# Both softmax types in 64-row tiles of TensorE, in a differential-attention block with routed experts

## Chip, cores, metric

One Trainium2 chip, one core of it. The metric is the device time of one launch in microseconds (us), median of three runs. Five engines work side by side: TensorE (PE; its weight loads are listed as PEld), VectorE (DVE), ScalarE (ACT), GpSimd (POOL) and SyncE (SP), whose queue starts most transfers (SPq). All times below are us of the profiled execution's own clock unless marked otherwise.

## The reference, cut to what matters

```python
x = X                                             # 32 batches x 256 rows x 128
h = layernorm(x) * (1 + ca) + sa                  # modulation per batch
Q, K, V = h @ W_q.T, h @ W_k.T, h @ W_v.T         # 16 heads, each 2*8 wide
A1 = Q[..., :8] @ K[..., :8].T / sqrt(8)          # the two softmax types
A2 = Q[..., 8:] @ K[..., 8:].T / sqrt(8)          # both with a causal mask
attn = softmax(A1) - lam * softmax(A2)
O = attn @ V
O = O / rms(O) * rms_scale * 0.2
x = x + ga * (concat(O) @ W_o.T)
h = layernorm(x) * (1 + cb) + sb
x = x + gb * top2_of_8_experts(h)                 # silu(h Wg) * (h Wu), then Wd
```

## The kernel before

The program has three stages: setup, attention over 32 batches, then the experts over 136 tiles of 128 routed rows. Attention is written as a software pipeline by hand. In iteration i every engine runs 16 head steps s = 0 to 15 and works at the same time on several batches: row maxima of batch i+1 (`b1`), exponentials and products with the values of batch i (`b2`), and earlier and later stages (projection of `bA` = i+2, outputs of `bC` = i-1, output projection of `bW` = i-2, routing of `bR` = i-3). What stands in a step is written out in the code of each engine; each engine executes strictly in that order, and semaphores (`wait(engine, event, batch, count)`) tie the engines together.

**Units.** The scores of a batch are computed in 24 units of one PSUM bank (128 x 512 fp32), numbered n = 0 to 23. An even step has one unit, an odd step two. They are computed twice. First for the row maxima: PE writes `p_max` (two banks), DVE takes the maxima (L1166, L1169), and the causal mask is added by one more matmul with the identity (L786, L795). Then, an iteration later, for the exponentials: PE writes `p_exp` (three banks), with minus the maximum as further rows of the product, ACT takes the exponential into `probs` (L988), POOL clears what the mask forbids (L1402). A query or key of 8 numbers is split into bf16 parts laid out as 6 slots, 48 rows. The queries of both types stand below each other (96 rows in `qt`), and `kt` has the keys of each type with zeros in the other type's rows. So one matmul works on 96 or 100 rows of which half are zeros.

**Values and outputs.** `outputs` (L835) multiplies a head pair g (0 to 7) of `probs` with `v` in four 32-column tiles of PE; pair g is visited at step 2g+3, the last one in step 1 of the next iteration. ACT copies each two pairs from `p_out` to `ot` (L978, `copy_outputs`, in steps 6, 10, 14 and 2), and PE turns them (L845, `outputs_to_rows`, in steps 11 and 14 for heads 0 to 7 and in steps 4 and 5 of the next iteration for heads 8 to 15).

**The path of the maxima.** For unit 0 of the next iteration SP does one after the other: wait for `l_ready` (POOL's L1408, `low_part`, step 6), nine stores of the parts (L707, L711), wait until they are saved, seven loads of queries and keys (L734, L740, `load_unit`), the store of the turned maxima (L747), wait until it is saved, and the load of them into `qt` (L750). PE's first exponential unit (L812) waits for that load, `nm_loaded`.

**Setup.** POOL fills `v` and zeroes `kt` (L1393); DVE waits for all 20 constant loads, two of them rows of ones for `kt` (L680).

## Time and profile before

| | us |
|---|---|
| three runs | 1588.79, 1586.29, 1580.92 |
| median | 1586.29 |
| the profiled execution: its time / its span | 1589.78 / 1588.0 |
| setup and filling of the pipeline, to about | 170 |
| steady attention iterations, about | 170 to 1030 |
| the rest of attention, tables, experts, final sum | 1030 to 1588 |

The page gives each engine's busy share over the whole span: PE 86%, weight loads 67%, DVE 74%, ACT 56%, POOL 55%. In the steady stretch the shares are higher and close to each other. A busy engine in such a pipeline may still be one that is waited for, and a short wait may be the one that sets the period, so the rows further down are read iteration by iteration. A line number with a matmul stands for a group; "96*128" are the rows and columns of the weights, "96x256" the streamed operand.

### The profile page before, as it was taken

The numbers are of one execution on the slowest core, as the hardware profiler recorded it, in microseconds if no ns is written. First come the engines' busy times: TensorE is split into PE (matmuls) and PEld (weight loads), VectorE is DVE, ScalarE is ACT, GpSimd is POOL, SyncE is SP. The second block draws the span as 40 slices with busy tenths as digits, with TensorE's granted clock in tenths as the row PEclk, the third lists the DMA queues.
The fourth block names the chain that finished last, engine by engine and source line by source line (L and its number), as shares of the span: only waits on it lengthen the run. The fifth ranks groups of instructions, "written<-read, shape, count | busy, mean of one in ns | idle before, by whom it ended". The sixth has DMA issues, their size and how long they took to land. (4 is left out here: it accounts for less than half of the span.)

```text
span 1588.0 us, 42685 instructions
## 1 busy us (share of the span) xinstructions
PE 1366.6 (86%) x13344; PEld 1063.3 (67%) x13345; DVE 1180.9 (74%) x3082; ACT 885.0 (56%) x1918; POOL 868.0 (55%) x1279
## 2 busy tenths in 40 slices
PE   1499999999999999999999999962599999999950
PEld 1266777767777776777777676641588888888850
DVE  4567888888888888788888887866666666666647
ACT  1166777777777777777777777652133333333310
POOL 2045577677767767676776776663233333333334
PEclk9999999999999999999999999985799999999985
DMA  6433443444344354444434533300211111111139
GB/s 213 123 100 83 129 118 94 118 118 114 103 126 121 92 133 110 103 110 118 122 88 120 128 98 90 87 24 14 59 48 43 46 43 42 46 43 45 42 94 295
DMA packets 176591, 152.61 MB, mean 96 GB/s; under 512 B 21491, under 2 KB 159097, under 8 KB 176036
## 3 DMA queue, kind: packets, MB, share of 16 engines
q1 hardware_dynamic: 159096, 123.07, 30.1%
q0 software_dynamic: 8448, 16.93, 3.3%
q10 hardware_dynamic: 8880, 10.49, 1.9%
q8 instruction: 92, 1.51, 0.4%
q14 instruction: 75, 0.61, 0.1%
HBM read 89.37 MB, written 61.55 MB: 95 GB/s over the span
## 5 line engine op out<-in xcount | busy, mean ns | idle before, releaser
L988 ACT ACTIVATE probs<-p_exp 128x512 f32<-128x512 f32 x768 | 446.5, 603 | 183.6 <-PE p_exp L812 164.3
L1402 POOL TENSOR_SCALAR_AFFINE_SELECT probs<-probs 128x256 f32<-128x256 f32 (+1 forms) x768 | 365.4, 485 | 286.4 <-ACT probs L988 278.3
L1166 DVE TENSOR_REDUCE mx<-p_max 128x2 f32<-128x512 f32 x512 | 351.4, 687 | 169.9 <-PE p_max L786 168.9
L647 POOL DMA_INDIRECT pair_out<-on,v x136 | 133.6, 982 | 284.7 <-ACT on L557 279.3
L784 PE MATMUL p_max<-kt,qt 96*128 96x256 bf16 x1024 | 198.6, 275 | 40.5 <-DMA kt<-k_parts 19.7
L835 PE MATMUL p_out<-probs,v 128*32 128x256 f32 (+1 forms) x4096 | 221.0, 333 | 14.0 <-POOL probs L1402 7.5
L812 PE MATMUL p_exp<-qt,kt 100*128 100x256 bf16 x1024 | 196.7, 273 | 16.8 <-DMA qt<-max_parts 14.0
L621 DVE TENSOR_TENSOR ot<-ot,p_max 128x512 f32<-128x512 f32 x136 | 93.5, 688 | 125.8 <-PE p_max L508 106.5
L1169 DVE TENSOR_REDUCE mx<-p_max 128x4 f32<-128x512 f32 x256 | 173.2, 676 | 2.1 <-PE p_max L795 2.0
L835 PEld LDWEIGHTS p_out<-probs,v 128*32 128x32 f32 x4096 | 112.4, 109 | 85.4 <-POOL probs L1402 24.4
L1449 POOL DMA_INDIRECT rows_sorted<-h,idx x128 | 137.4, 1074 | 50.7 <-ACT probs L988 28.6
L557 ACT ACTIVATE on<-p_exp,v 128x128 f32<-128x128 f32 x136 | 50.3, 370 | 195.7 <-PE p_exp L539 195.7
L539 PE MATMUL p_exp<-wd,rest 128*128 x1088 | 143.9, 275 | 0.9 <-ACT on L557 0.9
L784 PEld LDWEIGHTS p_max<-kt,qt 96*128 96x128 bf16 x1024 | 89.3, 100 | 81.5 <-DVE mx L1166 25.6
L786 PE MATMUL p_max<-mask,idb 128*128 128x256 bf16 x512 | 141.1, 276 | 0.0
L551 ACT ACTIVATE ot<-p_exp 128x512 f32<-128x512 f32 x136 | 81.6, 600 | 95.3 <-PE p_exp L508 95.3
L539 PEld LDWEIGHTS p_exp<-wd,rest 128*128 128x128 f32 x1088 | 132.2, 192 | 1.3 <-issue 1.3
L812 PEld LDWEIGHTS p_exp<-qt,kt 100*128 100x128 bf16 x1024 | 98.6, 99 | 36.7 <-DMA qt<-max_parts 18.9
L978 ACT ACTIVATE ot<-p_out,out_scale 128x256 f32<-128x256 f32 x256 | 107.1, 475 | 0.0
L792 PE MATMUL p_max<-kt,qt 96*128 96x128 bf16 x1024 | 101.5, 222 | 4.4 <-DVE mx L1166 2.0
L1408 POOL TENSOR_TENSOR part_l<-rest,part_m 128x512 bf16<-128x512 f32 x64 | 74.2, 1160 | 51.5 <-ACT part_m L1004 51.5
L818 PEld LDWEIGHTS p_exp<-qt,kt 100*128 100x128 bf16 x1024 | 79.8, 98 | 30.8 <-issue 1.1
(169 smaller groups left out, 2757.9 us busy)
## 6 DMA issues: line engine op xcount, KB each, us to landing
qt<-q_parts SPq DMA_DIRECT2D x64, 384.0 KB
q_parts<-part_h SPq DMA_DIRECT2D x96, 128.0 KB, 2.0
kt<-k_parts SPq DMA_DIRECT2D x128, 96.0 KB
v<-rows_sorted SPq DMA_DIRECT2D x136, 65.0 KB, 1.8
q_parts<-part_m SPq DMA_DIRECT2D x64, 128.0 KB, 2.0
kt<-k_parts SPq DMA_DIRECT2D x128, 64.0 KB
qt<-pair_out SPq DMA_DIRECT2D x32, 256.0 KB, 5.4
mods<-mod_rows SPq DMA_DIRECT2D x32, 192.0 KB
```

What stands on the lines that cost most here:

```text
L539: m = nc.tensor.matmul(p_down, hid_t[:, jd.c % 2, f * P:(f + 1) * P], wd[:, bass.ds(w0 + f * P, P)], start=(f == 0), stop=(f == FCH - 1))
L647: nc.gpsimd.indirect_dma_start(pair_out, bass.IndirectOffsetOnAxis(rows_in[:, j.slot, DIM:DIM + 1].bitcast(U32), 0), rows_out[:, j.slot, : ...
L784: nc.tensor.matmul(p_max[:, bank, t * SEQ:(t + 1) * SEQ], qt[0:QK_ROWS, slot, h8, P:SEQ], kt[0:QK_ROWS, slot, t, h8, :], start=(t == 0), s ...
L786: m = nc.tensor.matmul(p_max[:, bank, :].rearrange("p (t k) -> p t k", t=2)[:, :, P:SEQ], idb[:], mask4[:, 0:2, :], start=False, stop=True)
L812: m = nc.tensor.matmul(p_exp[:, bank, t * SEQ:(t + 1) * SEQ], kt[0:ALL_ROWS, slot, t, h8, 0:P], qt[0:ALL_ROWS, slot, h8, :], start=True, s ...
L835: m = nc.tensor.matmul(p_out[32 * j:32 * j + 32, g % 2, SEQ - n:SEQ], v[:, b.par, tile, 2 * g + j // 2, :], src, start=(tile == 0), stop=( ...
L978: m = nc.scalar.activation(ot[:, q // 2, 2 * (q % 2) + k, :], p_out[:, k, :], ACT.Copy, scale=out_scale[:, g:g + 1])
L988: nc.scalar.activation(probs[:, g % 2, k, :], p_exp[:, k, :], ACT.Exp, scale=SCALE).then_inc(exp_done.sem, 1)
L1166: m = V.reduce_max(mx[:, w, 1, :, h8:h8 + 1].rearrange("p t o -> p (t o)"), p_max[:, bank, :].rearrange("p (t k) -> p t k", t=2), AX.X, ne ...
L1169: m = V.reduce_max(mx[:, w, 0, :, h8 - 1:h8 + 1], p_max[:, bank, :].rearrange("p (t h k) -> p t h k", t=2, h=2), AX.X, negate=True)
L1402: G.affine_select(out=blocks, in_=blocks, compare_op=ALU.is_ge, fill=zero, base=0, pattern=[[0, 2 if k < 2 else 4], [1, P]], channel_multi ...
L1449: G.indirect_dma_start(rows_sorted, bass.IndirectOffsetOnAxis(idx[:, bR.par, k:k + 1].bitcast(U32), 0), h2[:, bR.par, k // NT, k % NT, :], ...
```

## The change

1. **Layout.** Each softmax type gets its own 64 rows of `qt` and `kt` (`LANE = 64`): 48 rows of parts, 2 `EDGES` rows, 2 rows of minus the maximum. `kt` has no second copy per type and no zeros any more. The edge rows add -1e30 in the one 64 x 64 block of each diagonal 128 x 128 block that lies wholly above the diagonal.
2. **Units.** A unit now holds one type: two heads of it (k = n % 6 below 4), or four heads' second-row blocks (k = 4, 5). The mask is two matmuls of 64 rows with triangular 64 x 64 blocks. `scores` interleaves, instruction by instruction, the maximum unit of one type (in one 64-row tile of PE) with the exponential unit of the other type (in the other tile).
3. **Values.** `probs` holds four heads (`quad`) per buffer; pair g is visited at step 2g+5, so pairs 6 and 7 are visited in steps 1 and 3 of the next iteration.
4. **Copies.** `copy_outputs` moves from steps 6, 10, 14, 2 to steps 8, 12, 0, 4, and the first `outputs_to_rows` from step 11 to step 12. The one in step 4 stays.
5. **Transfers.** `load_unit` issues eight loads instead of seven (two of queries, 48 rows each), `move_max` two stores (32 rows of 256 B) and two loads instead of one of each.
6. **Setup.** The zeroing of `kt` goes; the ones are no longer among the constants DVE waits for (18 instead of 20). Ten loads of ones and edge rows come in their place, eight of them behind a wait for POOL; PE waits for all ten.

```diff
+LANE = 64
+QK_ROWS = SLOTS * DH
+EDGES = 2
...
-            def scores_for_exp(b, h, n, tile):
...
+            def max_unit(b, n):
...
+                t, k, bank, slot, heads = n % 2, n % 6, n % 2, 2 * b.par + n // (NBANKS // 2), unit_heads(n)
+                rows = slice(LANE * t, LANE * t + SHIFT_AT)
...
+            def scores(bm, be, n):
+
+                for _ in itertools.zip_longest(max_unit(bm, n), exp_unit(be, n)):
+                    pass
...
-                        g = s // 2 - 1
+                    scores(b1, b2, n)
+                    if s % 2:
+                        scores(b1, b2, n + 1)
+                    if s % 2:
+                        g = s // 2 - 2
...
-                    if s == 11 and active(b2):
+                    if s == 12 and active(b2):
                         outputs_to_rows(i, b2, 0, 0, 0, 5)
...
-                    if s in (6, 10, 14) and active(b2):
-                        copy_outputs(b2, (s - 6) // 4)
-                    if s == 2 and active(bC):
+                    if s in (8, 12) and active(b2):
+                        copy_outputs(b2, (s - 8) // 4)
+                    if s == 0 and active(bC):
+                        copy_outputs(bC, 2)
+                    if s == 4 and active(bC):
                         copy_outputs(bC, 3)
...
-            G.memset(kt[0:QK_ROWS].rearrange("p a t h k -> p (a t h k)").bitcast(F32), 0.0)
```

TensorE, step 4 and the start of step 5, with the semaphores waited for. Before:

```order
L784 MATMUL p_max<-kt,qt 128x256 [waits max_done]
L784 MATMUL p_max<-kt,qt 128x256
L786 MATMUL p_max<-mask,idb 128x2x128
L812 MATMUL p_exp<-qt,kt 128x256 [waits exp_done]
L812 MATMUL p_exp<-qt,kt 128x256
L845 MATMUL p_mix<-idf,ot 128x128 [waits ot_ready,nmt_ready]
L845 MATMUL p_mix<-idf,ot 128x128 x3
L784 MATMUL p_max<-kt,qt 128x256 [waits max_done]
```

TensorE, the same place in the changed kernel:

```order
L813 MATMUL p_max<-kt,qt 128x256 [waits max_done]
L842 MATMUL p_exp<-qt,kt 128x256 [waits exp_done]
L813 MATMUL p_max<-kt,qt 128x256
L842 MATMUL p_exp<-qt,kt 128x256
L821 MATMUL p_max<-tri,idb 128x2x64
L821 MATMUL p_max<-tri,ids 128x2x64
L881 MATMUL p_mix<-idf,ot 128x128 [waits ot_ready,nmt_ready]
L881 MATMUL p_mix<-idf,ot 128x128 x3
L813 MATMUL p_max<-kt,qt 128x256 [waits max_done]
```

The two units are interleaved, and the mask takes two matmuls; the turning of `ot` stands where it stood, right behind unit 6.

ScalarE, from unit 0 (step 0) to unit 6 (step 4). Before:

```order
L988 ACTIVATE probs<-p_exp 128x512 [waits pv_done,exp_ps]
L1017 ACTIVATE ht<-p_mix,sa_t,ca_t 128x256 [waits v_ps,xt_ps]
L988 ACTIVATE probs<-p_exp 128x512 [waits exp_ps] x2
L1022 COPY ont<-p_mix 128x512 [waits ont_ps]
L1000 CAST part_h<-p_mix 128x512 [waits parts_saved,proj_ps]
L988 ACTIVATE probs<-p_exp 128x512 [waits pv_done,exp_ps]
L978 ACTIVATE ot<-p_out,out_scale 128x256 [waits ot_ps,pv_done]
L978 ACTIVATE ot<-p_out,out_scale 128x256
L988 ACTIVATE probs<-p_exp 128x512 [waits exp_ps] x2
L1004 CAST part_m<-rest 128x512 [waits r_ready]
L994 COPY nmt<-p_mix 32x256 [waits nm_saved,nm_ps]
L1000 CAST part_h<-p_mix 128x512 [waits parts_saved,proj_ps]
```

ScalarE, from unit 0 to the copies behind unit 6, changed, without the rows of steps 1 to 3:

```order
L1015 ACTIVATE probs<-p_exp 128x512 [waits pv_done,exp_ps]
L1043 ACTIVATE ht<-p_mix,sa_t,ca_t 128x256 [waits v_ps,xt_ps]
L1005 ACTIVATE ot<-p_out,out_scale 128x256 [waits ot_ps,pv_done]
L1005 ACTIVATE ot<-p_out,out_scale 128x256
L1015 ACTIVATE probs<-p_exp 128x512 [waits exp_ps] x2
...
L1026 CAST part_h<-p_mix 128x512 [waits parts_saved,proj_ps]
L1015 ACTIVATE probs<-p_exp 128x512 [waits pv_done,exp_ps]
L1005 ACTIVATE ot<-p_out,out_scale 128x256 [waits ot_ps,pv_done]
L1005 ACTIVATE ot<-p_out,out_scale 128x256
```

One pair of copies moved from behind unit 3 to behind unit 6, another from step 14 to behind unit 0.

SyncE, the transfers behind the nine stores (L734 to L750 before, L755 to L775 now). Before:

```order
L734 DMA qt<-q_parts 96x2048 [waits parts_saved,exp_ps]
L740 DMA kt<-k_parts 24x2048
L740 DMA kt<-k_parts 16x2048
L740 DMA kt<-k_parts 8x2048
L740 DMA kt<-k_parts 24x2048
L740 DMA kt<-k_parts 16x2048
L740 DMA kt<-k_parts 8x2048
L747 DMA max_parts<-nmt 32x256 [waits nmt_ready]
L750 DMA qt<-max_parts 4x2048 [waits nm_saved]
```

SyncE, the same transfers in the changed kernel:

```order
L755 DMA qt<-q_parts 48x2048 [waits parts_saved,exp_ps]
L760 DMA kt<-k_parts 24x2048
L760 DMA kt<-k_parts 16x2048
L760 DMA kt<-k_parts 8x2048
L755 DMA qt<-q_parts 48x2048
L760 DMA kt<-k_parts 24x2048
L760 DMA kt<-k_parts 16x2048
L760 DMA kt<-k_parts 8x2048
L769 DMA max_parts<-nmt 32x128 [waits nmt_ready]
L769 DMA max_parts<-nmt 32x128
L775 DMA qt<-max_parts 2x2048 [waits nm_saved]
L775 DMA qt<-max_parts 2x2048
```

Three more issues stand between the last store of the parts and the last load of the maxima.

## Rows read from the trace of the kernel before

**Rows 1.** Busy time by stretch: span, then PE, PEld, DVE, ACT, POOL, clock, DMA.

```profile
203.80:973.20 769.40, 732.02 (x8390) 547.72 (x8387) 649.33 (x1851) 581.78 (x1274) 548.61 (x876) 1.00 0.43 112
```

**Rows 2.** Groups by shape, 203.8 to 973.2: count, busy, mean ns, idle before, releasers.

```profile
L1166 DVE TENSOR_REDUCE mx<-p_max 128x2 f32<-128x512 f32 x400 | 274.7, 687 | 112.8 <-PE p_max L786 112.1
...
L1275 DVE TENSOR_TENSOR on_tok<-o,rstd 128x512 f32<-128x512 f32 x25 | 17.0, 680 | 0.0
```

**Rows 3.** Waits, 200 to 980: us in total, times, longest.

```profile
PEld p_exp L812 <- DMA qt<-max_parts: 13.1, 12, 2.6
```

**Rows 4.** Timeline of SyncE's queue, 469 to 476 and at 630: start, us, line, count.

```profile
469.07 0.33 SPq L734 DMA_DIRECT2D qt<-q_parts  x1
...
472.57 0.31 SPq L747 DMA_DIRECT2D max_parts<-nmt  x1
475.13 0.24 SPq L750 DMA_DIRECT2D qt<-max_parts  x1
...
630.13 0.24 SPq L750 DMA_DIRECT2D qt<-max_parts  x1
```

**Rows 5.** Timeline of PE, 447 to 460 and at 477.5: start, us, line, count.

```profile
447.53 0.39 PE L812 MATMUL p_exp<-qt,kt 100*128 100x256 bf16 x2 [0.48 <-issue]
...
449.30 0.86 PE L835 MATMUL p_out<-probs,v 128*32 128x256 f32 x16
...
456.60 0.60 PE L845 MATMUL p_mix<-idf,ot 128*128 128x128 f32 x4
457.04 0.38 PE L784 MATMUL p_max<-kt,qt 96*128 96x256 bf16 x2
457.26 0.27 PE L786 MATMUL p_max<-mask,idb 128*128 128x256 bf16 x1
457.37 0.38 PE L812 MATMUL p_exp<-qt,kt 100*128 100x256 bf16 x2
457.59 0.39 PE L792 MATMUL p_max<-kt,qt 96*128 96x128 bf16 x4
457.82 0.38 PE L795 MATMUL p_max<-mask,idb 128*128 128x512 bf16 x1
458.04 0.39 PE L818 MATMUL p_exp<-qt,kt 100*128 100x128 bf16 x4
458.35 0.86 PE L835 MATMUL p_out<-probs,v 128*32 128x256 f32 x16
...
459.63 0.38 PE L784 MATMUL p_max<-kt,qt 96*128 96x256 bf16 x2
...
477.50 0.38 PE L812 MATMUL p_exp<-qt,kt 100*128 100x256 bf16 x2
```

**Rows 6.** Timeline of POOL at 461.5: the second `low_part`.

```profile
461.52 1.16 POOL L1408 TENSOR_TENSOR part_l<-rest,part_m 128x512 bf16<-128x512 f32 x1
```

**Rows 7.** The step-0 wait of PE at 631.95 (timeline).

```profile
631.95 0.39 PE L812 MATMUL p_exp<-qt,kt 100*128 100x256 bf16 x2 [1.49 <-DMA qt<-max_parts]
```

**Rows 8.** Timeline of ACT, 448 to 461.

```profile
448.90 1.11 ACT L988 ACTIVATE probs<-p_exp 128x512 f32<-128x512 f32 x2
...
456.80 0.60 ACT L988 ACTIVATE probs<-p_exp 128x512 f32<-128x512 f32 x1
457.79 1.27 ACT L988 ACTIVATE probs<-p_exp 128x512 f32<-128x512 f32 x2 [0.39 <-PE p_exp L812]
...
460.39 0.60 ACT L988 ACTIVATE probs<-p_exp 128x512 f32<-128x512 f32 x1 [0.82 <-PE p_exp L812]
460.88 0.84 ACT L978 ACTIVATE ot<-p_out,out_scale 128x256 f32<-128x256 f32 x2
```

**Rows 9.** Timeline of setup, 9 to 19.

```profile
9.80 0.43 SPq L676 DMA_DIRECT2D fill<-in_filler  x1
...
18.22 0.49 DVE L1117 TENSOR_TENSOR rest<-rest 128x128 f32<-128x128 f32 x2 [7.88 <-DMA kt<-in_max_ones]
```

**Rows 10.** Busy time by stretch (columns as in rows 1), behind the wait of rows 7.

```profile
632.60:636.00 3.40, 3.40 (x30) 2.00 (x28) 1.86 (x3) 2.03 (x4) 2.35 (x5) 0.50 0.98 203
```

More of the change, by code:

```diff
@@ L261, in adaln_block @@
         nmt_ready = ev("nmt_ready", 2)
[L262 to L263 removed]
+        nm_saved = ev("nm_saved", 2 * 16 * NT)
+        nm_loaded = [ev(f"nm_loaded{w}", 32) for w in range(2)]
         exp_ps = ev("exp_ps", NBANKS)
@@ L797, in scores_for_max @@
-                m.then_inc(max_ps.sem, 1)
-            def scores_for_exp(b, h, n, tile):
-                w, h8, bank = h // HU, h % HU, n % 3
-                slot = 2 * b.par + w
+                for j, h in enumerate(heads):
+                    if k < 4:
+                        yield nc.tensor.matmul(p_max[:, bank, j * SEQ:(j + 1) * SEQ], qt[rows, slot, h, P:SEQ],
+                                               kt[rows, slot, h, :], start=(j == 0), stop=False)
+                    else:
+                        yield nc.tensor.matmul(p_max[:, bank, j * P:(j + 1) * P], qt[rows, slot, h, 0:P],
+                                               kt[rows, slot, h, 0:P], start=(j == 0), stop=False)
@@ new lines, in max_unit @@
+                blocks = p_max[:, bank, :].rearrange("p (j k) -> p j k", j=len(heads))
+                for half in range(2):
+                    c = (P if k < 4 else 0) + LANE * half
+                    m = nc.tensor.matmul(blocks[:, :, c:c + LANE], (idb if half == t else ids)[masks, :],
+                                         tri4[masks, 0:len(heads), :], start=False, stop=(half == 1))
+                    if half == 1:
+                        m.then_inc(max_ps.sem, 1)
+                    yield m
@@ L804, in scores_for_exp, with exp_unit @@
+            def exp_unit(b, n):
+                if not active(b):
+                    return
+                t, k, bank, slot, heads = 1 - n % 2, n % 6, n % 3, 2 * b.par + n // (NBANKS // 2), unit_heads(n)
+                rows = slice(LANE * t, LANE * t + ALL_ROWS)
                 if n in (0, NBANKS // 2):
-                    wait(pe, nm_loaded[w], b)
+                    wait(pe, nm_loaded[n // (NBANKS // 2)], b)
                 if n >= 3:
@@ L858, in max_to_rows @@
                 settle(pe)
-                pm = p_mix[:, 1, 0:P].bitcast(BF16)
-                for tile in range(NT):
-                    m = nc.tensor.transpose(pm[0:SHIFT_ROWS * HU, tile * P:(tile + 1) * P],
-                                            nm[:, w, 2 * tile:2 * tile + 2, :, :].rearrange("p t s h -> p (t s h)"), idb[:])
-                m.then_inc(nm_ps.sem, 1)
+                nc.tensor.transpose(p_mix[:, 1, 0:LANE].bitcast(BF16), nm[:, w, :], idb[:]).then_inc(nm_ps.sem, 1)
             def body(i):
```

200 lines of the change are left out of this document (101 added, 99 removed).

## The prediction

> **What bounds the kernel now.** I read the busy time by stretch first: in the steady stretch PE is busy for 732 of 769 us, DVE for 649, ACT for 582, POOL for 549 [rows 1]. That looks like a kernel bound by PE. But a busy PE counts the tails of its matmuls, so I went on to the period of an iteration. One `on_tok` stands in each; 25 of them lie in 769.4 us [rows 2], so an iteration takes **30.78 us** on average. The waits say that it isn't the same every time: in 12 of the 25, PE waited in step 0 for the load of the maxima [rows 3]. So I cut one iteration in which it did not wait, and looked at how near the load was.
>
> From PE's first exponential matmul at 447.53 to that of the next iteration at 477.50 are 29.97 us [rows 5]. **Leg A** runs over PE and ACT until POOL has made the last part, 461.52 + 1.16 = 462.68 [rows 6]: 15.15 us. **Leg B** is SyncE's: nine stores, seven loads, the store of the maxima at 472.57, their load at 475.13 [rows 4]. In another iteration such a load was issued at 630.13 and PE went on at 631.95 after a wait of 1.49 us [rows 4, 7], so landing takes 1.82 us. Here it landed at 476.95, only 0.55 us before PE came. So legs A and B together are a ring that sets the period in about half of the iterations and is within half a us of it in the others. What counts in this change is what it does to that ring, not PE's sum.
>
> **Scores in two tiles.** Streams follow each other at 0.11 us for 256 columns (457.04 to 457.26 is two), 0.055 for 128 (457.59 to 457.82 is four) and 0.22 for 512 [rows 5]. Before, an even step has 5 x 0.11 = 0.55 us and an odd one 1.22 (457.04 to the last of four at 458.04 + 0.22). The trace shows no two row tiles at work at once. The nearest row is L835, where 16 records, each 0.27 to 0.40 long, fit into 0.86 us [rows 5]: four column tiles do overlap. I take full overlap of two tiles, each tile in order. One new unit is then 0.11 + 0.11 + two masks of 0.055 = 0.33 us. Two in a row, the second starting in the other tile while the last mask runs, are 0.61; two with four blocks of 128, whose masks are 0.11 each, 0.83. The other end is no overlap: 0.55, 1.10, 1.32.
>
> **Changes of tile shape.** From L818's last stream at 458.26 to L835 at 458.35 PE stands still for 0.09 us [rows 5]. The new units differ in shape from the full-array matmuls around them, so an even step pays this twice more and an odd one once more; I take 0.10 each. An even step so goes from 0.55 to 0.53: nothing is won in it. Odd steps win 0.51 (steps 1, 5, 9, 13) or 0.29 (3, 7, 11, 15). Over 16 steps PE's saving is 3.4 us an iteration. The Trainium skill (TensorEngine Tiling, "Key Properties") says that tiles work independently and that a change of mode drains the engine. It gives no price for the drain; by independent tiles and a free drain the saving would be 5.8, by no overlap there would be a loss of 2.3.
>
> **The copies behind unit 0.** Pair 6 of the values in step 1 now waits for copies that ACT starts in step 0, behind its exponential and `ht`. ACT had finished these two at 448.90 [rows 8], 1.37 us after the start; two copies take 0.84 [rows 8], so PE can go on 2.26 us after the start with 0.05 for the signal. Before, L835 began 1.77 us after it (449.30) [rows 5]. **Leg A + 0.49.** Behind PE's wait stand everything of step 1 and unit 3, for which DVE waits.
>
> **The copies behind unit 6.** PE turns `ot` in step 4 right behind unit 6, as before, but the copies it needs now stand on ACT behind the exponential of that same unit. Until there PE wins 0.02 (unit 3), 0.29 (units 4, 5), 0.02 (unit 6) and 0.06 (one bf16 transpose less), so it arrives 0.49 - 0.39 = 0.10 later than before, at 456.70. The exponential of unit 6 began at 456.80 [rows 8] because ACT was at `part_h`, whose source now comes 0.12 later (0.49 - 0.02 - 0.29 - 0.06): 456.92. Exponential to next instruction is 0.49 (460.39 to 460.88), the copies 0.84, the signal 0.05 [rows 8]: PE turns `ot` at 458.30 instead of 456.60 [rows 5]. **A new wait of 1.60 us; leg A is now + 1.70.** Nothing hides it on PE, since the order is fixed; DVE has its own work for most of it. Units 7 and 8 then win 0.51. Unit 9's exponential started 0.76 behind the unit's first matmul (459.63 to 460.39) [rows 5, 8]; interleaved it starts 0.42 behind its own first matmul (457.37 to 457.79) [rows 5, 8], which is 0.02 behind the unit's, with 0.10 for the shape: 0.22 won. **Leg A + 0.97.** Step 12 has the same order and a like wait of about 1.6 us, but it lies after leg A, and DVE, which it delays by about 1 us, reaches unit 0 still ahead of the load; so I cost it at nothing. If leg B weren't there, it would be what comes last.
>
> **Leg B.** One more load of queries (0.33 to issue), one more store (0.31) and one more load of maxima (0.24) [rows 4]: 0.88 us if each counts in full. The lower end is 0.24: the store lands behind the traffic of the loads, 2.56 us after its issue here (472.57 to 475.13) [rows 4], and an issue before it may drown in that. Where the load was last I take 0.88, where it was 0.55 early, 0.33; by 12 and 13 of 25 that is **+ 0.6**. Bytes stay the same. In step 0 the wait now also stops the maximum unit, since the exponential's first matmul stands second in the interleaved order; DVE gets unit 0 later than it would have, which before it did not.
>
> **Setup.** DVE waited until 18.22 for the ones [rows 9]. The last of the other constants was issued at 9.80 [rows 9] and should be there by about 12 to 13; the zeroing goes too. The ten new loads have until PE starts. **- 5 us**; ends 0 and - 6.
>
> **Clock.** After the wait of rows 7 PE's granted clock stood at 0.50 (its 1.2 GHz level) for 3.4 us [rows 10]; with PE busy all through, that is 1.7 us of work lost. Two waits of 1.6 us in every iteration are like that one. Of the 12 waits of rows 3 hardly any cost a fall, so I take 4 falls in 30 iterations: **+ 7 us**; ends 0 and + 50.
>
> **Sum.** An iteration takes 30.78 + 0.97 + 0.6 = 32.35 us. About 30 have all stages, + 47 us. 1589.8 (profiled) + 47 - 5 + 7 = 1638.8. The profiled execution lay 3.5 above the median, so **1635 us**. With 0.9 us either way on the two legs together the forecast's own range is 1608 to 1662. Experts, tables and final sum keep their instructions.
>
> **Rivals.**
> - *The ring isn't lengthened (15%).* PE makes good its waits where it had waited before, and the new issues drown in the traffic. PE saves 3.4 and waits 0.5 + 1.6 + 1.6 = 3.7 more, nearly a draw; with 0 to 0.2 us an iteration and the setup's - 5 it ends at 1581 to 1587. For it: the DMA's time varies by more than 0.88. Against it: the waits come on top wherever PE sets leg A.
> - *DVE is fed at last, faster (8%).* DVE sat idle 112.8 us for PE [rows 2], 4.5 an iteration. If half of it goes, 1589.8 - 68 - 5 - 3.5 = 1513. It decides only if the waits in steps 4 and 12 stay under 0.5 us, which needs ACT to run ahead of PE; the semaphores forbid it. The Trainium skill (TensorEngine Tiling, "PSUM Bottleneck") warns that tiling speeds up TensorE but not the emptying of PSUM. DVE's and ACT's shapes stay as they are, so this caps the gain: all 4.5 gone would be 1446.
> - *No overlap (12%).* Row tiles run one after the other. Leg A becomes + 2.5: units 3, 4 and 5 take 0.2 + 0.2 longer before the same wait, so it ends at + 2.4, and behind it nothing is won. 30 x 3.1 = 93 in place of 47: 1681.
> - *The clock falls often (13%).* 15 falls instead of 4, each 1.7: 1654; at 30 falls 1679. It decides from one in three iterations on.
> - *The forecast: 52%.*
>
> **How the numbers follow.** What a measurement here tells from no change is about 0.5%, 8 us. Faster by more than that (below 1578): the second rival and a piece of the first, 12%. Within it: most of the first, 11%. Slower: forecast, no overlap, clock, 77%. The range leaves out the faster cases, the lowest end of the first rival and the worst of the clock: 1582 to 1690.
>
> **What would show it.** In the new timeline PE idles 1.4 to 2.0 us before the first matmul of `outputs_to_rows` in steps 4 and 12, released by ACT's copies, and 0.5 us or more before pair 6. The first-unit wait for the load of the maxima appears in most iterations. An even step's scores take 0.33 us of streams and an odd one's 0.61 or 0.83; if they take 0.55 and 1.1 or more, the tiles don't overlap. The period of `on_tok` is 32.0 to 33.0. DVE's first product of lambdas starts at about 13. I am wrong if the period is below 31.2: then ring or waits aren't where I put them.

## The result and the profile after

The changed kernel took **1718.4 us** (median of 4 runs, 1711.1 to 1731.7) against 1587.5 for the kernel before (4 runs), timed side by side with it: a ratio of 1.084, 95% interval 1.077 to 1.092. It is slower, as forecast, but by 131 us where the forecast had 49, and it lies above the range of 1582 to 1690. The profiled execution has a span of 1715.3 us, against 1588.0 before.

Busy time by stretch, after: span, then PE, PEld, DVE, ACT, POOL, granted clock, DMA share, GB/s. It answers to [rows 1].

```profile
203.80:1030.00 826.20, 677.55 (x8584) 435.64 (x8579) 641.97 (x1775) 548.55 (x1224) 523.31 (x840) 0.91 0.44 101
```

PE was busy 95% of the stretch before and is busy 82% now; the mean granted clock fell from 1.00 to 0.91. `on_tok` gives the period, as in [rows 2]: the groups by shape and, of its line, the count with the first and the last start:

```profile
L1304 DVE TENSOR_TENSOR on_tok<-o,rstd x26: 680/685/697, 226.4 to 1092.8; 128x512 f32<-128x512 f32 x26
```

(1092.8 - 226.4) / 25 = 34.66 us, where [rows 2] gave 30.78 and the forecast was 32.35. DVE's reductions still take 0.68 us each, but the engine waits for PE before them. Two groups from 210 to 1030 us, columns as in [rows 2]:

```profile
L1197 DVE TENSOR_REDUCE mx<-p_max 128x2 f32<-128x512 f32 x381 | 257.6, 684 | 166.2 <-PE p_max L821 161.9
L881 PE MATMUL p_mix<-idf,ot 128*128 128x128 f32 x376 | 68.0, 309 | 68.8 <-ACT ot L1005 68.8
```

PE waited 68.8 us before turning `ot` (before the change none), and DVE's idle time for PE went from 4.5 to 166.2 / 23.7 = 7.0 us an iteration. Waits of PE from 200 to 1000 us (us in total, times, longest), to be read beside [rows 3]:

```profile
PE p_mix L881 <- ACT ot L1005: 69.0, 47, 1.6
PE p_exp L842 <- DMA qt<-max_parts: 16.2, 14, 2.2
PE p_out L871 <- ACT ot L1005: 14.1, 21, 1.1
```

One iteration at full clock, PE's timeline (start, us, line, count, idle before and its releaser). It begins with the exponential's first matmul at 950.87 and answers to [rows 5]:

```profile
950.87 0.27 PE L842 MATMUL p_exp<-qt,kt 52*128 52x256 bf16 x1
...
953.76 0.86 PE L871 MATMUL p_out<-probs,v 128*32 128x256 f32 x16 [0.82 <-ACT ot L1005]
...
956.00 0.28 PE L813 MATMUL p_max<-kt,qt 50*128 50x256 bf16 x1
956.01 0.28 PE L842 MATMUL p_exp<-qt,kt 52*128 52x256 bf16 x1
956.12 0.27 PE L813 MATMUL p_max<-kt,qt 50*128 50x256 bf16 x1
956.13 0.27 PE L842 MATMUL p_exp<-qt,kt 52*128 52x256 bf16 x1
956.23 0.22 PE L821 MATMUL p_max<-tri,ids 64*128 64x128 bf16 x1
956.29 0.21 PE L821 MATMUL p_max<-tri,idb 64*128 64x128 bf16 x1
956.44 1.16 PE L933 MATMUL p_mix<-wo,ont 128*128 128x128 f32 x8
957.53 0.23 PE L816 MATMUL p_max<-kt,qt 50*128 50x128 bf16 x1
...
958.31 0.86 PE L871 MATMUL p_out<-probs,v 128*32 128x256 f32 x16
...
962.48 0.63 PE L881 MATMUL p_mix<-idf,ot 128*128 128x128 f32 x4 [1.56 <-ACT ot L1005]
```

Three things are to be seen. The matmuls of the two types start together (956.00 and 956.01): **the two row tiles do run at once**, and the step's scores take 956.00 to 956.34, the 0.33 us that the prediction put in. The odd steps behind it are no longer than forecast either: step 3 of this iteration takes 957.53 to 958.31 with the change of shape at its end, 0.78 us for 0.93, and step 5 takes 0.66 for 0.71. Pair 6 waits 0.82 us in step 1. And the turning in step 4 waits 1.56 us for the copies that stand on ACT behind the exponential of the same unit. The rest of this iteration's ring, POOL's last part, SyncE's queue and PE's next first matmul, beside [rows 6] and [rows 4]:

```profile
966.64 1.16 POOL L1442 TENSOR_TENSOR part_l<-rest,part_m 128x512 bf16<-128x512 f32 x1
...
967.83 1.43 SPq L727 DMA_DIRECT2D q_parts<-part_h  x3
...
977.11 0.77 SPq L769 DMA_DIRECT2D max_parts<-nmt  x2
981.36 0.53 SPq L775 DMA_DIRECT2D qt<-max_parts  x2
...
983.41 0.28 PE L842 MATMUL p_exp<-qt,kt 52*128 52x256 bf16 x1 [0.39 <-DMA qt<-max_parts]
```

Leg A is 950.87 to 967.80, 16.9 us; leg B is 967.80 to 983.41, 15.6 us.

The legs of 24 iterations (the 5th to the 28th) say where the period's growth of 3.71 us came from. An iteration without a fall of the clock (23 of 24 before, 5 of 24 after) takes 15.37 + 15.34 = 30.71 us before and 16.95 + 16.54 = 33.49 after. The other 0.93 are the falls: the records have PE's clock at its lower level for 0.14 us an iteration before and for 5.8 after. This split between legs and clock is a rough one. In all five iterations without a fall ACT's first exponential starts late, 0.86 to 1.13 us behind PE's matmul, where in 14 of the 24 it starts 0.42 to 0.47 behind. In the three of those 14 in which the clock was up all through leg A, leg A is 16.40.

| profiled execution, us | before | after |
|---|---|---|
| first exponential matmul of batch 0 | 81.9 | 91.3 |
| from it to that of batch 31 | 952.2 | 1064.3 |
| from there to the end | 553.8 | 559.7 |
| period, 24 iterations | 30.79 | 34.50 |
| leg A / leg B without falls | 15.37 / 15.34 | 16.95 / 16.54 |

### The profile page after: what moved, and what is told of

It is laid out like the page before. It is cut to its first block and busy times, and to the rows that moved or that the text cites. A ratio compares the mean times of both kernels' runs of the same rounds, so it can differ in the third digit from the quotient of the medians.

```text
span 1715.3 us, 44177 instructions
## 1 busy us (share of the span) xinstructions
PE 1340.8 (78%) x14048; PEld 947.2 (55%) x14049; DVE 1195.6 (70%) x3089; ACT 872.6 (51%) x1918; POOL 861.5 (50%) x1283
## 3 DMA queue, kind: packets, MB, share of 16 engines
q0 software_dynamic: 8448, 16.93, 3.2%
## 5 line engine op out<-in xcount | busy, mean ns | idle before, releaser
L1197 DVE TENSOR_REDUCE mx<-p_max 128x2 f32<-128x512 f32 (+1 forms) x768 | 516.2, 682 | 266.1 <-PE p_max L821 260.2
L871 PE MATMUL p_out<-probs,v 128*32 128x256 f32 (+1 forms) x4096 | 251.0, 369 | 25.5 <-ACT ot L1005 18.1
L813 PE MATMUL p_max<-kt,qt 50*128 50x256 bf16 x1024 | 204.0, 296 | 70.3 <-DVE mx L1197 45.6
L842 PE MATMUL p_exp<-qt,kt 52*128 52x256 bf16 x1024 | 210.0, 294 | 30.1 <-DMA qt<-max_parts 30.0
L821 PE MATMUL p_max<-tri,idb 64*128 64x128 bf16 (+1 forms) x768 | 184.7, 247 | 0.0
L821 PE MATMUL p_max<-tri,ids 64*128 64x128 bf16 (+1 forms) x768 | 183.0, 247 | 0.0
L634 DVE TENSOR_TENSOR ot<-ot,p_max 128x512 f32<-128x512 f32 x136 | 93.5, 688 | 123.5 <-PE p_max L521 106.8
L881 PE MATMUL p_mix<-idf,ot 128*128 128x128 f32 x512 | 93.3, 311 | 93.5 <-ACT ot L1005 93.5
L813 PEld LDWEIGHTS p_max<-kt,qt 50*128 50x128 bf16 x1024 | 69.8, 97 | 167.1 <-DVE mx L1197 71.2
L881 PEld LDWEIGHTS p_mix<-idf,ot 128*128 128x128 f32 x512 | 60.9, 155 | 116.1 <-issue 113.0
L845 PE MATMUL p_exp<-qt,kt 52*128 52x128 bf16 x1024 | 100.8, 222 | 0.0
```

Source lines behind the costliest of these rows:

```text
L813: yield nc.tensor.matmul(p_max[:, bank, j * SEQ:(j + 1) * SEQ], qt[rows, slot, h, P:SEQ], kt[rows, slot, h, :], start=(j == 0), stop=False)
L821: m = nc.tensor.matmul(blocks[:, :, c:c + LANE], (idb if half == t else ids)[masks, :], tri4[masks, 0:len(heads), :], start=False, stop=(h ...
L842: m = nc.tensor.matmul(p_exp[:, bank, j * SEQ:(j + 1) * SEQ], kt[rows, slot, h, 0:P], qt[rows, slot, h, :], start=True, stop=True)
L871: m = nc.tensor.matmul(p_out[32 * j:32 * j + 32, pair, SEQ - n:SEQ], v[:, b.par, tile, 2 * g + head, :], src, start=(tile == 0), stop=(til ...
L881: m = nc.tensor.transpose(p_mix[:, bank, g * P:(g + 1) * P], ot[:, w, g, tile * P:(tile + 1) * P], idf[:])
L1197: V.reduce_max(mx[:, w, tile, t, heads[0]:heads[-1] + 1], p_max[:, bank, :].rearrange("p (h k) -> p h k", h=len(heads)), AX.X, negate=True ...
```

## The experiments

Every kernel is timed side by side with the kernel before on the same chip, and its ratio is against that. There are three such groups, in which the kernel before took 1587.1, 1589.2 and 1591.8 us; the changed kernel itself was not timed again in them. So a difference of a few us between two experiments says nothing. The period and legs given are means over the same 24 iterations of the profiled execution.

**Undo the delay of the copies alone.** ACT copies one step earlier, behind the other work of the step.

```diff
-                    if s in (8, 12) and active(b2):
-                        copy_outputs(b2, (s - 8) // 4)
-                    if s == 0 and active(bC):
-                        copy_outputs(bC, 2)
-                    if s == 4 and active(bC):
-                        copy_outputs(bC, 3)
...
+                    if s in (7, 11, 15) and active(b2):
+                        copy_outputs(b2, (s - 7) // 4)
+                    if s == 3 and active(bC):
+                        copy_outputs(bC, 3)
```

> The changed kernel with ACT's copies of the values one step earlier again: at the end of steps 7, 11, 15 and 3, in place of steps 8, 12, 0 and 4. Theory 'late copies': PE waited in steps 1, 4 and 12 for ACT's copies (93.5 us before L881, 14.7 before pair 6), they lengthen leg A at full clock by 1.6 us an iteration and they bring the clock down about once an iteration (5.8 us at the half level in each, about 1.0 us of time). Without them an iteration goes from 34.5 to 31.6 to 32.2, the granted clock of 200 to 1000 us from 0.91 to 0.97 or more, the time from 1718 to 1640 (1625 to 1665). What stays above the kernel before is leg B. Rival 'the tiles themselves': two tiles at work draw the clock down and changes of shape cost more than 0.1 us; then the waits go but the clock stays near 0.91 and the time stays above 1690.

Measured: 1672.9 us (ratio 1.056, 1.053 to 1.058), outside both expectations. Leg A without a fall is 15.20, shorter by 1.75, but the period is 32.83, since the clock stands at its lower level for 4.95 us of each iteration: nearly as much as with the late copies. And the delay was not undone: both waits before the turning of `ot` stayed, in every one of the 24 iterations, at 1.07 us in step 4 (for 1.56) and 0.53 in step 12 (for 1.37), 38 us of 70 in all. (The 93.5 us of the expectation are those of the whole execution, not of these iterations.) The wait in step 4, in PE's and in ACT's timeline:

```profile
264.90 0.63 PE L881 MATMUL p_mix<-idf,ot 128*128 128x128 f32 x4 [1.07 <-ACT ot L1005]
```

```profile
263.44 0.58 ACT L1026 CAST part_h<-p_mix 128x512 bf16<-128x512 f32 x1 [0.66 <-PE p_mix L887]
263.92 0.84 ACT L1005 ACTIVATE ot<-p_out,out_scale 128x256 f32<-128x256 f32 x2
264.64 0.61 ACT L1015 ACTIVATE probs<-p_exp 128x512 f32<-128x512 f32 x1
```

I had put the step-3 copies behind `part_h`, which itself waits for PE, so they still came late. The late copies cost leg A 1.7 us or more. On the clock this run decides nothing, since more than half of the waiting was still there; the kernel with the placed copies, below, does.

**Fill PE's waits, leave their ends.** Eleven matmuls, whose result is overwritten, ahead of the wait in steps 4 and 12.

```diff
                 mix_free(pe, i, bank, turn)
+                if tile == 0:
+                    for _ in range(11):
+                        nc.tensor.matmul(p_mix[:, bank, 0:SEQ], idb[:], tri4[:], start=True, stop=True)
                 wait(pe, ot_ready, b, 2 * (w + 1))
```

> The changed kernel with 11 extra matmuls of 256 columns (1.2 us at full clock, 0.11 each) on PE right before its wait for ACT's copies in steps 4 and 12; their results are overwritten. The waits keep their ends, but PE is busy in them. It tells what the waits do to the clock from what they do to the path. Theory 'late copies': the falls of the clock vanish for the most part (granted clock of 200 to 1000 us 0.97 or more), an iteration goes from 34.5 to 33.5, the length of the iterations without a fall, and the time to 1688 (1675 to 1700). Rival 'the tiles themselves draw the clock down': the clock stays at 0.91 and the time at 1718 (1705 to 1735).

Measured: 1690.5 us (ratio 1.066, 1.062 to 1.070), 28 us less than the changed kernel. Busy time by stretch, here and in the changed kernel:

```profile
400.00:600.00 200.00, 180.07 (x2298) 118.60 (x2297) 164.57 (x447) 139.07 (x310) 129.82 (x212) 0.97 0.45 105
```

```profile
400.00:600.00 200.00, 163.13 (x2036) 104.94 (x2032) 150.01 (x414) 129.25 (x287) 122.94 (x197) 0.91 0.43 96
```

More work on PE and less time. The lower level is down from 5.8 to 3.1 us an iteration: those two waits made about half of the falls. Where the falls went shows it for each of the two. Of the 30 falls between 203 and 1030 us in the changed kernel, 7 come at the end of the wait of step 4 or up to 1.4 us behind it, and 3 come 1.5 us behind that of step 12; with the waits filled none is left in either place. Another 8 come before the wait of step 12 begins, 2.5 to 3.5 us ahead of its end; 4 of those are left. Of the 20 falls in all, 16 lie within 3 us of the iteration's start, at the wait for the maxima and that of pair 6. The period is 33.71, as expected; that the falls would vanish for the most part did not come true (0.96 from 200 to 1000 us for 0.97 or more).

**Price leg B alone**, in the kernel before: its transfers cut as in the changed one.

```diff
-                sp.dma_start(max_parts[bass.ds(b.n, 1), w].rearrange("a r h k -> (a r h) k"),
-                             nmt[:, w, :]).then_inc(nm_saved.sem, 16)
+                for t in range(NT):
+                    sp.dma_start(max_parts[bass.ds(b.n, 1), w, :, :, t * P:(t + 1) * P].rearrange("a r h k -> (a r h) k"),
+                                 nmt[:, w, t * P:(t + 1) * P]).then_inc(nm_saved.sem, 16)
```

> The kernel before with the transfers cut as in the changed one: the load of the queries in two (48 rows each), the store of the maxima in two (128 columns each), their load in two (2 rows each). Bytes and all else as before. It prices leg B alone. Theory: three more issues of SyncE between the last part and PE's first exponential: leg B goes from 15.3 to 16.5 us as in the changed kernel, and since the ring is the limit in half of the iterations and within 0.5 us in the others the period goes from 30.8 to 31.6 (31.3 to 31.9): 1612 (1603 to 1624). Rival 'the issues drown in the traffic': 1588, within 8 us.

Measured: 1613.2 us (ratio 1.015, 1.012 to 1.018), as the ring has it: + 26 us, a period of 31.55. Leg B is 15.93, where 16.5 was expected: half of the growth in the changed kernel. Part of the 26 us is the clock: it fell 5 times for 2, and in the iterations without a fall (17 here, 23 before) the period is 31.08 for 30.71. PE's waits for the maxima, 200 to 1000 us, beside [rows 3]:

```profile
PEld p_exp L815 <- DMA qt<-max_parts: 32.7, 24, 3.2
```

24 iterations now wait where 12 did. Three more issues of SyncE a half batch, with not a byte more, cost 26 us with what they do to the clock.

**Setup: the loads of x first.**

```diff
+            for j in range(2):
+                sp.dma_start(xres[:, j * SEQ:(j + 1) * SEQ].rearrange("p (t c) -> p t c", t=NT),
+                             x[j:j + 1].rearrange("a (t p) c -> p (a t) c", p=P)).then_inc(x_loaded[j].sem, 16)
             for t in range(2):
                 at = LANE * t + SHIFT_AT
```

> The changed kernel with the two first loads of x issued before the ten loads of ones and edges. Theory: DVE stood 10.2 us before its first statistics (33.95 us) for x, which was issued at 16.97 behind those ten and behind ACT's 6 MB of weights; issued at about 10.3 us it lands by 20, so the first exponential of PE comes 5 to 9 us earlier (91.3 to about 84) and the time is 1711 (1707 to 1715). Rival: the edges, then next in line, or the first projections hold the start where it is: within 3 us of 1718.

Measured: 1721.8 us (ratio 1.086, 1.084 to 1.089), no difference from the changed kernel and outside both expectations. That the order of the loads holds up x is shown; that it is worth anything isn't. DVE's first statistics, first in the changed kernel and then here:

```profile
33.95 0.49 DVE L1238 BATCH_NORM_STATS2 stats<-xres 128x6 f32<-128x128 f32 x2 [10.18 <-DMA xres<-in_x]
```

```profile
23.95 0.49 DVE L1241 BATCH_NORM_STATS2 stats<-xres 128x6 f32<-128x128 f32 x2 [0.17 <-DVE out_scale L1191]
```

10 us won there; at PE's first exponential matmul 4.1 are left (87.2 for 91.3; the expectation had 5 to 9), and of those the runs, which spread over 24 us, show nothing.

**Put the copies where ACT waits anyway**, and turn the first half of `ot` behind the scores of step 13.

```diff
+                    if s in (8, 12) and active(b2):
+                        copy_outputs(b2, (s - 8) // 4)
+                    if s == 0 and active(bC):
+                        copy_outputs(bC, 2)
                     if active(b2):
                         exp_bank(b2, s + s // 2)
...
+                    if s == 3 and active(bC):
+                        copy_outputs(bC, 3)
                     if s == 3 and active(bA):
                         high_part(bA, 1)
```

> The changed kernel with ACT's copies placed where ACT waits anyway: ahead of the exponentials of steps 0, 8 and 12, in step 3 between the copy of the maxima and part_h; and PE turns the first half of ot in step 13 behind the scores, not in step 12. It asks whether leg A is long only through the place of the copies. Theory 'place': the three waits of PE for ACT fall below 0.3 us each, leg A at full clock comes to 14.7 to 15.2 (16.95 in the changed kernel, 15.2 with the copies a step early), leg B stays 16.2 to 16.6, an iteration takes 31.5 to 32.5 with the falls of the clock that PE's idle time in front of the ring still brings: 1655 (1635 to 1675). Rival 'shape and interleaving cost leg A too': leg A stays above 15.8 and the time at 1690 or more.

Measured: **1623.9 us** (ratio 1.023, 1.020 to 1.026), 94 us less than the changed kernel and better than expected. PE's wait for ACT's copies is gone from the list of waits. The falls are not: the clock stands at its lower level for 4.93 us an iteration, for 5.83 in the changed kernel. **That the late copies alone bring the clock down is refuted here**, since none of their waits is left; 13 of the 22 falls now lie 20.7 to 23.7 us behind the first exponential matmul. Leg A is 14.89 with the falls in it and 14.13 in the three iterations without one, 1.2 less than in the kernel before. So with tiles and interleaved units leg A can be shorter than before, once the copies are out of the way. Leg B (16.50) is the changed kernel's. PE in one iteration from 436.06 on, turning in step 4 with no wait:

```profile
442.25 0.86 PE L871 MATMUL p_out<-probs,v 128*32 128x256 f32 x16
...
444.79 0.66 PE L881 MATMUL p_mix<-idf,ot 128*128 128x128 f32 x4
```

**Shorten leg B by early stores**, in the changed kernel and in the kernel before: high parts are stored once they are made, then the middle ones, then the last.

```diff
-                    wait(sp, l_ready, b)
-                    for s, part in enumerate(Q_SLOTS):
-                        buf = (part_h, part_m, part_l)[part]
+                    for part, (buf, made) in enumerate(((part_h, h_ready), (part_m, m_ready), (part_l, l_ready))):
+                        wait(sp, made, b)
+                        for s in [s for s in range(SLOTS) if Q_SLOTS[s] == part]:
```

> The changed kernel, with SyncE storing the high parts once they are made and the middle ones once these are, not all nine behind the last part. Two stores are left behind the last part. It shortens leg B alone. Theory 'the ring of legs A and B sets the period': seven issues of 0.3 us leave leg B, so an iteration goes from 34.5 to 32.6 (32.2 to 33.2), the time from 1718 to 1660 (1645 to 1680). Rival 'PE's waits and the clock set it, the load was only next in line': 1700 or more.

> The same early stores in the kernel before. Theory 'ring': in half of the iterations the load of the maxima comes last, in the others it is within 0.5 us; with leg B 2 us shorter PE's own order and DVE set the period, 30.8 goes to 29.9 (29.5 to 30.3) and the time to 1560 (1548 to 1572). Rival 'the ring is not the limit before': 1587 within 8.

Measured: in the changed kernel 1681.7 us (ratio 1.060, 1.057 to 1.064), between the two expectations; in the kernel before 1563.5 (ratio 0.984, 0.982 to 0.986), as expected, at a period of 30.38. In the changed kernel the load of the maxima was now early; SyncE and PE, timelines:

```profile
536.01 0.53 SPq L774 DMA_DIRECT2D qt<-max_parts  x2
...
540.35 0.27 PE L812 MATMUL p_max<-kt,qt 50*128 50x256 bf16 x1 [0.49 <-issue]
540.48 0.27 PE L841 MATMUL p_exp<-qt,kt 52*128 52x256 bf16 x1
```

The load was issued 4.5 us before its user came, and no wait for it is left in the list. Yet the period only went from 34.50 to 34.10. So in the changed kernel **the ring was not the only limit**: PE's own order with its waits for ACT and the falls of the clock takes 34 us, right behind it. This kernel also prices a fall by itself, since no load is waited for: an iteration takes 32.02 us on average where the clock stays up (7 of 24), 33.41 with 3.4 us at the lower level (9 of 24) and 36.84 with 13.7 us (7 of 24). So 34.10 is 32.0 at full clock and 2.1 of falls. Most of the 37 us came outside these 24 iterations: the other seven iterations, ahead of these and behind them, took 25 us less (from 80 to 200 us the clock was 1.00 for 0.91), and the first fill 5.

**All together.** Placed copies, early stores, x first; then with eight extra matmuls in step 9, where PE stands for DVE.

```diff
                     if s == 9 and active(b1):
                         max_to_rows(i, b1, 0, 6)
+                    if s == 9 and active(b2):
+                        mix_free(pe, i, 0, 5)
+                        for _ in range(8):
+                            nc.tensor.matmul(p_mix[:, 0, 0:SEQ], idb[:], tri4[:], start=True, stop=True)
```

> The changed kernel with the placed copies, the early stores and the loads of x first. Theory 'ring': with leg A as before and leg B 2 us shorter than in the changed kernel the period is 29.7 (29.0 to 30.5) and the time 1570 (1550 to 1600); the two tiles then win something, since PE's streams are no longer in the way. Rival 'the clock': a PE with more idle time runs 5 to 10% of the stretch at the half level, and the iteration stays above 30.8: 1600 to 1640, slower than before with early stores.

> The combined kernel with eight extra matmuls of 256 columns (0.9 us at full clock) on PE in step 9 behind the turning of the maxima, where PE stands 0.9 us for DVE; their results are overwritten. In the combined kernel the clock fell 21.6 us behind the first exponential in nearly every iteration and stayed at the half level for 6.8 us. Theory 'the idle time ahead of step 10 brings the clock down': the granted clock of 200 to 1000 us goes from 0.90 to 0.98 or more, the iteration from 30.6 to 29.7 (what the iterations without a fall took), the time from 1553 to 1528 (1515 to 1540). Rival 'other waits bring it down next, or PE is not what sets the period there': 1553 within 8.

Measured: 1553.3 us (ratio 0.977, 0.974 to 0.981) and, with the extra matmuls, **1542.3 us** (ratio 0.969, 0.966 to 0.973), the fastest kernel of this study, faster than the kernel before and than the kernel before with early stores. The profiled execution without the extra matmuls is the slowest of its six, 1568.6 us. In it 22 of the 24 falls came 21.5 us behind the first exponential matmul or a little later. PE ahead of one such fall, and the stretch before it and the one behind:

```profile
480.83 0.28 PE L815 MATMUL p_max<-kt,qt 50*128 50x256 bf16 x1 [0.88 <-DVE mx L1199]
```

```profile
479.70:483.10 3.40, 2.52 (x43) 1.52 (x43) 3.37 (x8) 2.35 (x7) 1.46 (x5) 1.00 0.72 154
483.10:486.50 3.40, 2.96 (x31) 1.71 (x24) 3.40 (x15) 2.41 (x7) 1.42 (x3) 0.51 0.48 87
```

With the extra matmuls the clock of 400 to 600 us is 0.99 where it was 0.90, and the period 29.50 where it was 30.55:

```profile
400.00:600.00 200.00, 184.09 (x2469) 120.74 (x2462) 172.30 (x495) 155.89 (x347) 148.67 (x238) 0.99 0.51 119
```

The gain in the median, 11 us, is less than the 25 expected; the two profiled executions differ by 21. The six executions without the extra matmuls say why. Sorted, with the mean granted clock of the whole execution:

| us | 1546.1 | 1546.3 | 1552.9 | 1553.7 | 1562.2 | 1568.6 |
|---|---|---|---|---|---|---|
| clock | 0.954 | 0.954 | 0.943 | 0.941 | 0.923 | 0.900 |

The time goes with the clock, and two of them kept it as well as the kernel with the extra matmuls (0.946 to 0.956, 1540.8 to 1547.4 us). So a fall in nearly every iteration is what the profiled execution had and not what the kernel always has, and the extra matmuls seem to make the good case the rule. The two kernels were timed on different chips, but their ratios to the kernel before lie apart.

**One store of the maxima**, with their order in memory changed so that one transfer takes all 64 rows; the two loads then gather runs of 128 elements.

```diff
-                for tile in range(NT):
-                    sp.dma_start(max_parts[bass.ds(b.n, 1), w, :, :, :, tile * P:(tile + 1) * P]
+                sp.dma_start(max_parts[bass.ds(b.n, 1), w].rearrange("a c t s h k -> (a c t s h) k"),
+                             nmt[:, w, :]).then_inc(nm_saved.sem, 16)
...
+                    sp.dma_start(qt[at:at + SHIFTS, 2 * b.par + w, :, :].rearrange("p h (c k) -> p h c k", c=NT),
```

> The kernel with the placed copies, the maxima stored by one transfer of 64 rows in place of two of 32 (the order in memory is changed for it, the two loads stay). It measures a part of leg B where leg A is short. Theory 'leg B sets the period there': an issue of 0.35 us less and the landing no later: an iteration goes from 31.4 to 31.0 (30.7 to 31.1), the time from 1624 to 1611 (1602 to 1616). Rival 'the store lands behind the traffic of the loads anyway': 1624 within 5.

> All that helped in one kernel: placed copies, early stores, x first, one store of the maxima, the extra matmuls in step 9. There the load of the maxima lands before PE comes, so by the ring it gives nothing on top of the extra matmuls: 1528 (1515 to 1540), the same as combined_fill within 5. If the load is still last in some iterations it gives up to 5 us more.

Measured: 1666.3 us (ratio 1.048, 1.044 to 1.051), 42 us slower than the kernel with the placed copies (the profiled executions differ by 32): a miss of both theories. I had costed the store and forgotten the loads. SyncE's queue, with one store first and then with two:

```profile
541.31 0.51 SPq L767 DMA_DIRECT2D max_parts<-nmt  x1
544.54 1.25 SPq L772 DMA_DIRECT2D qt<-max_parts  x2
```

```profile
525.06 0.77 SPq L769 DMA_DIRECT2D max_parts<-nmt  x2
529.11 0.53 SPq L775 DMA_DIRECT2D qt<-max_parts  x2
```

The two loads take 1.25 us to issue for 0.53, and from the last load's issue to PE's first exponential it is 2.31 us on average for 1.79 (2.30 for 1.75 where PE did wait for it). The Trainium skill (DMA: Bandwidth & Descriptors, "Why small descriptors are slow") gives each packet of a transfer with HBM a fixed overhead, 27% on Trainium2 where the pieces are of 256 bytes, as here. The trace agrees in the sign, since the landing takes 0.5 us longer for the same bytes; the issue, 0.72 us longer, the section doesn't speak of. Leg B grew by 0.56 us on average, the period by 0.90; in the iterations without a fall, few as they are (6 here, 3 there), leg B and the period both grew by 0.97 and leg A not at all. Where leg B is the limit, what is added to it is paid in full. In the kernel with everything, where the load has slack, the same edit costs 8 us: 1550.3 (ratio 0.975, 0.971 to 0.979) for 1542.3, more than the 5 allowed for, though the period is 29.50 in both. PE does wait for the load again in it, 13 times from 200 to 1000 us, at most 1.0 us. Where the 8 us are stays open.

## Why the prediction was right in sign and wrong in size

| term, us | forecast | measured | by |
|---|---|---|---|
| leg A, per iteration | + 0.97 | + 1.58 | iterations without a fall |
| leg B, per iteration | + 0.6 | + 1.20 | the same |
| clock, per iteration | + 0.23 | + 0.93 | the rest of the period's growth |
| setup and first fill | - 5 | + 9.4 | first exponential matmul |
| drain and experts | 0 | + 5.9 | the rest of the span |

The period grew by 3.71 in those 24 iterations, and all 31 periods by 112.1; with 9.4 and 5.9 that is the span's 127. The forecast had 49. Over 31 iterations the clock's term missed by 22 us, leg A's and leg B's by 19 each; the setup's missed by 14 and the rest by 6. So no step failed alone. The signs named ahead came true but for the period: 15 of the 24 iterations end in a wait of PE for the maxima, and PE waits before the turning in both steps of all 24.

**What bounds the kernel before: right.** The ring of legs A and B was there. Three more issues in leg B made the kernel before 1.5% slower, early stores made it 1.6% faster.

**Tiles, shapes: right.** Full overlap, 0.33 us a unit, 0.1 at a change of shape (956.34 to 956.44), and two units in an odd step a little less than forecast. The rival without overlap falls. (Its own account gives leg A as + 2.5 and as + 2.4; nothing hangs on which.)

**Leg A: the mechanism right, the size short by 0.6.** In the iteration shown leg A is 16.93 us, 1.78 more than the 15.15 of the iteration in [rows 5] and [rows 6]. Wait of 1.56 in step 4 for 1.60 forecast. From pair 6 to the turning it is 962.48 - 953.76 = 8.72 us, where [rows 5] have 456.60 - 449.30 = 7.30: + 1.42 for the + 1.21 of the steps. The larger part failed at the first step: pair 6 comes 2.89 us behind the first exponential matmul in this iteration, for 2.26 forecast. ACT, timeline:

```profile
951.08 0.87 ACT L1112 ACTIVATE h<-xres,neg_mr,rstd 128x128 f32<-128x128 f32 x2
951.85 0.58 ACT L1015 ACTIVATE probs<-p_exp 128x512 f32<-128x512 f32 x1
952.33 0.56 ACT L1043 ACTIVATE ht<-p_mix,sa_t,ca_t 128x256 f32<-128x256 f32 x1
952.78 0.84 ACT L1005 ACTIVATE ot<-p_out,out_scale 128x256 f32<-128x256 f32 x2
```

ACT's first exponential started 0.98 us behind PE's matmul, since ACT was still at `h` of step 15. In the iteration that I cut it started at 0.44, which is the least of the 24 to 0.01; their mean is 0.78. I worked from the fastest case of ACT. That is not the whole of it, and ACT isn't later in the changed kernel in general: its mean there is 0.65, while the five iterations without a fall, from which the + 1.58 is read, have 1.00. Compared like with like, ACT early in both, leg A is 16.40 for 15.15, + 1.25 for the + 0.97 of the forecast.

**Leg B: short by half.** In it each of the three issues counts in full (0.34, 0.34 and 0.27 us, 0.95 for + 0.6); the remaining 0.25 is a slower issue of the loads and a later landing of the store. My discount of 0.55 us for half of the iterations did not hold: 15 of the 24 now end in a wait of PE for the load. Cut the same way in the kernel before, they made leg B only 0.57 longer, because the store then landed sooner (3.42 us from the last store of the maxima to their last load, for 3.69). In the changed kernel it did not (4.08), nor in the kernel with the placed copies (3.98). Why the store lands later there stays open.

**Clock: the step that failed most, if narrowly.** I took 4 falls in 30 iterations and gave 15 or more a chance of 13%; there were 30 from 203 to 1030 us, twelve of them of 6.8 us and the others of 3.4, with a mean of 5.8 us an iteration at the lower level. I had priced falls by the wait in [rows 10] and judged the waits of 1.6 us to be nearly harmless, since those of [rows 3] had been. It was the number of falls that I had wrong and not the price of one: 1.7 us for 3.4 at the lower level, where the changed kernel with early stores has 1.4 (33.41 - 32.02). What I left out is, I think, that the change itself takes work out of PE's timeline, so that a wait which the kernel before bore is one too many now. Putting work back took falls away twice, which fits it; that it is the lack of work, and not what the work is, no run shows. In its version with cut transfers the kernel before bore even this, a wait of 1.57 us and PE busy for 1.83 of 3.4 us, and kept its clock; in the profiled execution of the combined kernel a wait of 0.88 us with PE busy for 2.52 of 3.4 us came ahead of a fall. The row of the former:

```profile
773.00:776.40 3.40, 1.83 (x20) 1.43 (x18) 3.06 (x7) 2.13 (x6) 3.19 (x5) 1.00 0.47 140
```

So PE's busy share in these two stretches doesn't tell them apart. The scores' matmuls use half of the rows of the array now; whether that is what does it wasn't tried, and the cause of the many falls stays open. Of the two rivals on the clock that the runs opposed, neither held alone: filling two waits took nearly half of the lower level's time away, removing all waits for the copies only a sixth of it (5.83 to 4.93 us an iteration).

**Setup: the wrong sign.** DVE's first product came at 12.02 as forecast for about 13, and the 5 us were then lost again at x. SyncE issues it behind the ten new loads (16.97 for 10.94 us), after ACT's loads of the experts' weights. I had priced the ten loads by when PE needs them, not by what stands behind them in the queue. Of the 9.4 us at the first exponential matmul, loading x first takes back 4.1; where the other 5.3 come from stays open.

**Step 12 at nothing: wrong.** Its wait is nearly half of the 69.0 us above, 3 of the 30 falls come right behind it and are gone once it is filled, and it stands in PE's own order. The prediction had said that this order comes last if leg B weren't there; with early stores the changed kernel shows it at 34 us with the falls and 32 without. And in 9 of the 24 iterations of the changed kernel PE did not wait for the load, so there PE's own order set the period already.

**DVE fed faster: at best in the last kernels, and not shown to be the tiles.** With the waits gone and leg B short the changed kernel is ahead, but not by much: 1553.3 us for the kernel before's 1563.5 with the same early stores, 1542.3 with the clock held up. It has the placed copies, the later turning and x first besides, and none of these was tried in the kernel before; so how much of the 10 to 21 us the tiles won isn't known. DVE then is busy for 172.3 of 200 us, 25 of the 29.5 of a period; its reductions take 0.68 us as ever. The prediction cited the Trainium skill (TensorEngine Tiling (Array Packing), "PSUM Bottleneck") for this cap, and the runs agree in that the reading of PSUM got no shorter; that DVE is what limits the last kernels wasn't tried.

**Where the 131 us are,** as far as runs tell: 94 go when the copies are placed and the turning moved (their waits above all: the period drops by 3.12 us and leg A by 3.00, while most of the falls stay); 26 is what the three transfers cost in the kernel before; 9 is the later start, by the profile. That these make 129 is in part luck. They are prices from three different kernels, loading x first won nothing in the median, and what the tiles save at PE would stand against them; the kernel with the placed copies still has the clock at its lower level for 4.93 us an iteration.

## What to carry to other kernels

A copy that frees nobody early should stand where its engine waits anyway, and not between a producer and the wait of the very engine that it feeds: three such places and one turning right behind cost 94 us here, and a placement by reading who waits for whom won them back. In a ring over several engines and a queue, an extra issue in the queue can be paid every turn, bytes or no bytes; look first at which of its transfers could leave before the last part is ready. When a change makes TensorE's work shorter, ask what its clock will do with the idle time, and try filling it. And look at the clock of every execution before reading much into the one that was profiled.

## What the runs showed that I had not expected

- Work added to PE made the kernel faster: 22 matmuls an iteration took 28 us off (1718.4 to 1690.5), eight took off 11 (1553.3 to 1542.3, on different chips), it seems by steadying the clock.
- In one execution of the combined kernel a wait of 0.88 us was followed by a fall of 6.8 us in nearly every iteration, where the kernel before with cut transfers kept its clock through one of 1.57. Two other executions of the same combined kernel kept a mean clock of 0.954 for its 0.900.
- Loads of the same bytes in runs of 128 elements, not of 2048, took 0.6 us each to issue on SyncE's queue, not 0.25.
